# Moving a bias addition, row sends, plan pieces and normalisations between the queues of a fused cross-attention and expert kernel

## The reference

```python
def xattn(ctx, tgt, mask):            # 8 heads of 16
    k, v = split(ctx @ W_src.T + b_src) * mask
    q = (tgt @ W_tgt.T + b_tgt) * mask
    attn = softmax(where(mask == 0, -inf, q @ k.T / 4))
    return concat([tgt, attn @ v]) @ W_out.T + b_out

def experts(x):                       # 8 experts, top 2 of each token
    p = softmax(x @ router.T); topv, topi = top_k(p, 2); topv /= topv.sum()
    return sum over the two picks of topv * (gelu(x @ w1[e]) @ w2[e])

x = x + tanh(g_xattn) * xattn(ctx, layernorm(x), mask)
x = x + tanh(g_ffn) * experts(layernorm(x))
```

## Time and profile before

| what | value |
|---|---|
| median of 3 runs | 326.61 us (326.29 to 327.12) |
| profiled execution, its own time | 324.83 us |
| its span, first to last instruction | 323.0 us |
| PE busy | 291.3 us (90%) |
| POOL busy | 220.7 us (68%) |
| DVE busy | 210.2 us (65%) |
| ACT busy | 193.9 us (60%) |
| granted TensorE clock, mean | 0.986 |

### The profile page before, as it was taken

How to read it: one execution, slowest core, us unless ns; L and a number is a source line. 1 busy time by engine, 2 the same in 40 slices (tenths; PEclk the granted TensorE clock), 3 DMA queues, 4 the chain that set the end, 5 groups by cost and what they waited for, 6 DMA issues and landing times.

```text
span 323.0 us, 10882 instructions
## 1 busy us (share of the span) xinstructions
PE 291.3 (90%) x3529; PEld 262.8 (81%) x3529; DVE 210.2 (65%) x886; ACT 193.9 (60%) x502; POOL 220.7 (68%) x301
## 2 busy tenths in 40 slices
PE   8799999998989999897788999999999999999920
PEld 3687787887879778776568998989999999999920
DVE  2758677698888868689567897359533443335653
ACT  3486869788797877867675448474444444444400
POOL 3745445443788888888555788788788888756860
PEclk9999999999999999999999999999999999999995
DMA  6635703113141211860234213213434333349346
GB/s 205 193 116 161 224 30 94 44 33 82 54 133 35 68 58 44 237 161 27 61 95 117 70 53 86 85 60 90 112 92 112 99 98 99 86 147 297 100 134 195
DMA packets 41236, 34.60 MB, mean 107 GB/s; under 512 B 5044, under 2 KB 36950, under 8 KB 41184
## 3 DMA queue, kind: packets, MB, share of 16 engines
q1 hardware_dynamic: 32608, 23.10, 25.8%
q0 software_dynamic: 4320, 8.47, 7.9%
q10 hardware_dynamic: 4256, 2.36, 2.5%
HBM read 22.35 MB, written 12.01 MB: 106 GB/s over the span
## 4 chain that ended last, share of the span: by engine, by line
PE 51%; POOL 23%; issue 14%; DVE 4%; ACT 3%; DMA 2%; POOLq 0%; ACTq 0%; DVEq 0%; SPq 0%
PE ps_sc L1622 16%; POOL rows L657 11%; PE ps_proj L1635 8%; PE ps_o L1635 7%; POOL kblk L598 3%; PE ps_o L1581 2%; POOL kblkr L595 2%; PE ps_proj L1516 2%; PE ps_o L1419 2%; PE ps_proj L1519 2%; POOL picked L675 2%; PE ps_sc L1465 2%; POOL xs L642 2%; POOL rs L614 2%; PE ps_sc L1460 1%
## 5 line engine op out<-in xcount | busy, mean ns | idle before, releaser
L675 POOL DMA_INDIRECT picked<-yo,xg x71 | 71.6, 1008 | 16.2 <-issue 11.2
L1622 PE MATMUL ps_sc<-xt,w1c 128*128 128x128 f32 x568 | 75.3, 276 | 1.8 <-ACT xt L846 1.2
L657 POOL DMA_INDIRECT rows<-xr,posi x64 | 63.4, 990 | 18.0 <-issue 17.4
L1622 PEld LDWEIGHTS ps_sc<-xt,w1c 128*128 128x128 f32 x568 | 69.0, 192 | 2.5 <-ACT xt L846 1.5
L855 ACT ACTIVATE probT<-ps_sc 128x512 f32<-128x512 f32 x71 | 42.4, 597 | 41.3 <-PE ps_sc L1622 41.3
L751 ACT ACTIVATE probT<-ps_sc,pencol 128x512 f32<-128x512 f32 x64 | 43.6, 683 | 18.7 <-PE ps_sc L1479 12.1
L1247 DVE TENSOR_REDUCE rowmax<-ps_sc 128x4 f32<-128x512 f32 x64 | 43.8, 685 | 13.9 <-PE ps_sc L1479 11.9
L595 POOL TENSOR_TENSOR kblkr<-kT,headcol 128x256 fp32r<-128x256 f32 x32 | 19.7, 616 | 35.5 <-ACT kT L788 35.2
L1635 PE MATMUL ps_proj<-w2s,probT 128*128 x288 | 38.0, 275 | 0.0
L1635 PE MATMUL ps_o<-w2s,probT 128*128 x280 | 37.0, 275 | 0.0
L1357 DVE COPY w1c<-w1s 128x512 f32 x71 | 32.0, 454 | 5.5 <-issue 3.4
(11 more groups left out here) (169 smaller groups left out, 605.9 us busy)
## 6 DMA issues: line engine op xcount, KB each, us to landing
xg<-rows SPq DMA_DIRECT2D x71, 65.0 KB, 1.9
ctxs<-ctxT SPq DMA_DIRECT2D x32, 128.0 KB, 2.2
xs<-x SPq DMA_DIRECT2D x8, 256.0 KB, 3.6
maskbc<-mask SPq DMA_DIRECT2D x8, 256.0 KB, 4.1
w1s<-w SPq DMA_DIRECT2D x4, 512.0 KB, 3.8
w2s<-w SPq DMA_DIRECT2D x8, 256.0 KB, 4.8
maskbc<-picked SPq DMA_DIRECT2D x4, 512.0 KB, 5.8
out<-xs ACTq DMA_DIRECT2D x6, 256.0 KB, 2.3
```

Source lines behind the costliest of these rows:

```text
L657: nc.gpsimd.indirect_dma_start(out=rows, out_offset=bass.IndirectOffsetOnAxis(ap=posi[:, i, pick, b:b + 1], axis=0), in_=xr[:, i, pick, b, ...
L675: nc.gpsimd.indirect_dma_start(out=picked, out_offset=bass.IndirectOffsetOnAxis(ap=xg[:, r, D + 1:D + 2].bitcast(I32), axis=0), in_=yo[:, ...
L1622: last = nc.tensor.matmul(ps_score[j % DEEP][:, c * 128:(c + 1) * 128], w1c[:, j % DEEP, c * 128:(c + 1) * 128], xt[:, j % XRING, :], star ...
```

## The change

1. On POOL the bias addition of every group now stands ahead of that step's `pen` and sends at k = 3. Before, it stood behind the sends for all groups but the first.
2. The sends of G = 3 go 3, 2 and 3 at steps (8, 1), (8, 2) and (8, 3), where they went 2, 2, 2 and 2 at (8, 1) to (9, 0). Those of G = 4 go 6 and 2 at (9, 1) and (9, 2), where they went 2 each at (9, 1), (9, 2), (9, 3) and (10, 0).
3. The first plan's five pieces go to (8, 0); (8, 1) twice; (9, 0) twice. They stood one each at (8, 0) to (9, 0).
4. ACT normalises G = 6 one sequence to a slot, in slots 2 to 5. Before, all four stood in step (9, 3), ahead of slot 3.
5. On DVE, at steps (9, 0) and (9, 1), the NEAR maxima come ahead of the reciprocal and product (L1265, L1268) of another sequence.

```diff
+SENDS_OF = {3: (range(0), range(0, 3), range(3, 5), range(5, 8)),
+            4: (range(0), range(0, 6), range(6, 8), range(0))}
-AHEAD = (10, 2)
...
     (POOL, step)
-                if k == 3 and G == 0:
+                if k == 3 and G is not None:
                     ... xs += bout_g, then s_xb
...
-                    scatter(G, SENDS[k])
-                G = group(g, 0)
-                if k == 3 and G is not None and G > 0:
-                    pool.wait_ge(s_xn, GROUP * G + GROUP)
-                    nc.gpsimd.tensor_tensor(xs[...], xs[...], bout_g[...], ALU.add).then_inc(s_xb, 1)
+                    scatter(G, SENDS_OF.get(G, SENDS)[k])
...
     (ACT, step and slot)
-                if k == 3 and G is not None and g != AHEAD[0]:
+                if k == 3 and G is not None and (g, 2) not in STEPS[MIXED:]:
                     normalise_again(G, range(GROUP))
...
-                b = n - slot_at(*AHEAD) - 2
-                if 0 <= b < GROUP:
-                    normalise_again(AHEAD[0] - LAG_OUT, (b,))
+                for g, k in STEPS[MIXED:]:
+                    b = n - slot_at(g, k) - 2
+                    if k == 2 and group(g, LAG_OUT) is not None and 0 <= b < GROUP:
+                        normalise_again(g - LAG_OUT, (b,))
...
     (DVE, step)
+                if n is not None and g > GROUPS:      # ahead of reciprocal and product
+                    highest(n, NEAR, s_max)
...
-                if n is not None:
+                if n is not None and g <= GROUPS:
                     highest(n, NEAR, s_max)
...
-                piece = {(8, 0): 0, (8, 1): 1, (8, 2): 2, (8, 3): 3, (9, 0): 4}.get((g, k))
+                for piece in {(8, 0): (0,), (8, 1): (1, 2), (9, 0): (3, 4)}.get((g, k), ()):
```

More of the change, by code:

```diff
@@ L637, in step @@
                 if G is not None and G <= STAGES[0]:
-                    scatter(G, SENDS[k])
-                G = group(g, 0)
-                if k == 3 and G is not None and G > 0:
-                    pool.wait_ge(s_xn, GROUP * G + GROUP)
[L642 to L645, removed]
+                    scatter(G, SENDS_OF.get(G, SENDS)[k])
             def scatter(G, sends):
                 i = outbox(G)[0]
-                if sends[0] == 0:
+                if 0 in sends:
                     pool.wait_ge(s_pos, POS * G + POS)
@@ L1258, in step @@
                     highest(n, FAR, s_max_far)
+                n = sequence(g, k, LAG_SCORE + 1)
+                if n is not None and g > GROUPS:
+                    wait(dve, s_exp_near, n)
+                    highest(n, NEAR, s_max)
                 n = sequence(g, k, LAG_O)
@@ L1332, in step @@
                     parts[0]()
-                piece = {(8, 0): 0, (8, 1): 1, (8, 2): 2, (8, 3): 3, (9, 0): 4}.get((g, k))
-                if piece is not None:
+                for piece in {(8, 0): (0,), (8, 1): (1, 2), (9, 0): (3, 4)}.get((g, k), ()):
                     first_pieces[piece]()
```

## The result

The changed kernel takes 332.73 us (median of 4 executions, 330.74 to 335.17), the kernel before beside it 326.45 us: ratio 1.0189, 95% interval 1.0151 to 1.0228. It is slower, outside the forecast's range. The profiled execution took 332.87 us; its span is 331.1 us instead of 323.0, at a mean granted clock of TensorE of 0.961 instead of 0.986.

A forecast was written before the change was run, and what follows sets the result against it. POOL is full, and its late bias addition reaches PE through DVE's waits. 1.91 + 0.1 - 1.39 + 0.3 - 0.2 = 0.7 us sooner: median 326.61 to 325.9 us, range 325.0 to 326.9, over the cases 324.3 to 327.3.

The forecast's parts named there:

- Part 1, the gain: Steps (7,0) to (7,1) and (8,0) to (8,1): DVE's waits for POOL's addition go, 0.84 and 1.07, together 1.91 us.
- The first wait: The first of DVE's three waits for POOL's addition, 1.1 us long: its removal gives PE 0.1, bounds 0 and 1.1.
- Part 1, the price: At (6,3) and (7,3) the earlier addition catches DVE's tw, 0.56 and 0.83 us late, 1.39 lost in all.
- Parts 2 to 4: Plan pieces and NEAR 0.3 us sooner; regrouped sends of G = 3 and G = 4 nothing; ACT's normalisation 0.2 later.
- the six sends: At (9,1), four more sends take 5.04 us where POOL idled 4.94; rs of G = 6 0.1 late, costing nothing.
- the forecast 0.2: At (10,0) PE waits some 0.2 us for the last normalised rows of G = 6; bounds 0 and 0.6.
- The trade forecast for the moved pieces: Two pieces leave (8,3), giving up to 0.69 us, and lengthen (8,1), costing 0 to 1.36, taken at 0.6.
- No price: Rival: tw slips past the addition or its delay is made up; 2.1 us won, 324.5 us; chance 0.35.
- the sign named for it: In the changed profile, tw at 0.16 us at both (6,3) and (7,3) would mean 324.5 us is near.
- Slower by keys: Rival: DVE's small operations caught behind POOL's keys at (8,1) to (8,3), up to 0.62 us each; chance 0.12.
- Stretched sends: Rival: sends pulled forward run much longer beside DVE, delaying rs of G = 6; up to 328.8 us; chance 0.02.
- Does nothing: Rival: POOL's period of 19.73 us rules and PE only waits elsewhere, for keys or inverse roots; 326.6 us; chance 0.07.

The follow-up runs named there:

- the wait for the selection: Kernel before with the bias addition ahead of the sends, but waiting for DVE's sum of the selections (sel_b): 326.38 us, ratio 0.9996.
- the addition alone: Kernel before with only the bias addition moved ahead of the sends: 333.0 us, ratio 1.0172.
- PE kept busy: Changed kernel with twelve unused matmuls of ones on PE ahead of rank, where PE waits for the held selection: 328.36 us, ratio 1.006.

## Why the prediction was wrong

**Part 1, the gain, was right.** Forecast 0.84 and 1.07 us, measured 0.83 and 1.06, and no wait of DVE for the addition is left. The first wait, taken at 0.1, gave 0.13 where the clock was held.

**Part 1, the price, is the step that failed.** The prediction has the addition start when kblk ends and catch tw at (6,3) and (7,3), 1.39 us. The mechanism was right, and with the wait for the selection it measured 0.64 + 0.84 = 1.48 us. Without the wait it was 5.15 us: wrong were the operation, the length and the number of places.

- The place (5,3) was left out. There tsum already stood against the key copies before the change, 0.71 us instead of 0.16, and the addition right behind them made that 2.48.
- The phase was taken from before. There sel of (6,3) started at 110.76 us, ahead of kblkr at 111.99. The hold at (5,3) made DVE later than POOL: with the clock held, sel stood 1.82 us later than before, at 112.58, and kblkr 0.74, at 112.73. In the changed kernel, with the clock fallen, both came another 1.5 us later, sel at 114.10 and kblkr at 114.24.
- The length was that of the addition, 1.29 us. It is that of the run, 0.62 + 0.62 + 1.26 less small overlaps: 2.4.

The SBUF — State Buffer page of the Trainium skill (section "SBUF: two separate sides") has whichever of the two starts first keep the shared ports for its whole instruction. The traces agree that DVE waits, but here the hold went through three instructions, 2.48 to 2.64 us, and tsum at (5,3) was held although it starts in the trace at 92.06 us, ahead of kblkr at 92.12.

**The clock had no term at all.** It took 4.4 us, more than half of the loss against a kernel before whose clock holds: 332.73 - 325.2 = 7.5 us, made of 4.4 for the clock and 328.36 - 325.06 = 3.3 for the addition without the wait against the addition with it; all else together is 0.1 the other way. The sum is rough, since these medians were taken beside kernels before of 326.45 to 327.10 us. The idle time ahead of the first fall was new: 1.47 us at (6,0), where PE's longest idle time in the profile of before is 0.45. That PE stands idle for 2.16 us near 155 us was in the timeline of before; that the clock was near its fall there could not be read from one profile in which it did not fall.

**Parts 2 to 4** were forecast at 0.1 us sooner in all, and measured 0.24% slower, with an interval that includes no change. With the clock held and the addition behind the wait for the selection they are within the noise: 325.06 against 324.84. In the changed kernel the six sends left 3.62 us of POOL's idle time, where none was forecast, for DVE came still later; with the clock held and the addition behind that wait none was left. PE's 0.17 us at (10,0) was the forecast 0.2. The trade forecast for the moved pieces is seen in the steps: (8,1) to (8,2) took 4.86 us instead of 4.51, (8,2) to (8,3) 4.11 instead of 4.68.

**The rivals.** No price: tw was at 0.16 us, the sign named for it, but because the hold had fallen earlier; the sign was not enough. Slower by keys: right that DVE caught behind POOL's keys would decide, wrong in place, (8,1) to (8,3), and in what puts them in the way; sel at (8,3) took 0.86 us. Stretched sends: not one longer than 1.197 us. Does nothing: no.

## What to carry to other kernels

Before an operation of POOL is moved up against others of its own, look for every DVE operation with two SBUF operands near the whole run, and for copies and scalar operations between SBUF tiles, at each place that the loop repeats, and shift DVE's times by the holds already found before looking at the next. Part such a run with a wait: 0.15 us of gap bought back 5 us here, of the hold and of the clock together. And where PE already idles for one or two microseconds, price a further wait also at the lower clock of the stretch behind it, and look at the granted clock of several executions before calling a stretch safe.

## What the runs showed of the hardware

DVE and POOL met not only at semaphores. DVE's operations on two SBUF operands were held through what was left of a run of three POOL operations that stood ready, 1.4 to 2.6 us. Where two operations stood, DVE got in after the first. What decides at such a boundary was not settled: with the addition halved, DVE got in ahead of the last operation at two places of three, with the whole addition at none of nine (the changed kernel, the addition alone, PE kept busy).

Operations on one operand were not safe either. DVE's operations that read PSUM (rowmax 0.68 us) and its statistics of xs (0.29) took no longer inside an operation of POOL than away from it. But in the changed kernel a copy, 0.36 us in the kernel before, took 0.57 and ended just behind kblk (97.92 + 0.61 = 98.53), and a scalar operation, 0.16 us elsewhere, took 0.74 and ended just behind kblkr (109.28 + 0.61 = 109.89):
```profile
97.98 0.57 DVE L1043 COPY xr<-integers 128x8 int32<-128x8 int32 x1
...
109.19 0.74 DVE L901 TENSOR_SCALAR ve<-mv 128x4 f32<-128x4 f32 x1
```
DVE waited beside sends too: sel at (5,3), and tw with the addition halved, ended only 0.05 to 0.14 us behind a send with another POOL operation ready after it. Elsewhere DVE ran on: in the kernel before, the update of the counts at 95.07 us took 0.16 amid a send with the addition right behind it. What decides this was not tested.

Matmuls whose result nobody uses, 1.5 to 1.7 us of them in idle time, held the granted clock at 1.00 where it else fell to 0.50 for some 3 and 10 us.
